# TensorE takes its rows of x straight from the store at a register's address, instead of from VectorE's copies

## The reference, cut to what matters

```python
def _propagate(all_emb, rows, cols, vals):
    acc = all_emb
    x = all_emb
    for _ in range(N_LAYERS):                      # 3
        x = jax.ops.segment_sum(vals[:, None] * x[cols], rows, num_segments=N_NODES)
        acc = acc + x
    return acc / (N_LAYERS + 1)
...
users_emb = all_users[users] + _upsample_nearest(mm_users[users])
items_emb = all_items + _upsample_nearest(mm_items)
rating = users_emb @ items_emb.T
rating = rating + bias_user[users] + bias_item.T
return jax.nn.sigmoid(rating)
```

## Time and profile before

| | |
|---|---|
| median of the runs | 7006.35 us (6999.16 to 7008.19) |
| the profiled execution: span | 7404.3 us |
| mean granted TensorE clock in it | 0.665 |
| VectorE (DVE) busy | 6190.8 us, 84% |
| TensorE (PE) busy | 4555.1 us, 62% |
| ScalarE (ACT) busy | 4518.3 us, 61% |
| GpSimd (POOL) busy | 2314.9 us, 31% |

### The profile page before, as it was taken

The page is one execution under the profiler, slowest core; times in us unless marked ns, Lnnn a source line. Parts: engine busy times, 40 slices in busy tenths (PEclk is TensorE's granted clock), DMA queues, the critical chain, the costliest instruction groups (busy, mean ns, idle before and its releaser), DMA issues.

```text
span 7404.3 us, 186636 instructions
## 1 busy us (share of the span) xinstructions
PE 4555.1 (62%) x58016; PEld 3947.8 (53%) x58020; DVE 6190.8 (84%) x15385; ACT 4518.3 (61%) x10708; POOL 2314.9 (31%) x2100
## 2 busy tenths in 40 slices
PE   5300111037777777886666666788666666678879
PEld 4200111036666666885555555688555555568854
DVE  9999999988888888998777777899877777789970
ACT  0155444345555557997555555799655555579976
POOL 0144344024544441001555555100155555510000
PEclk9755555566766666665777777655577777755569
DMA  9400000025555555554444444455344444445536
GB/s 345 159 0 0 0 0 0 0 73 148 152 149 149 149 149 136 143 145 106 136 138 136 142 138 139 133 145 146 108 138 137 136 140 138 137 131 145 147 107 241
DMA packets 750539, 918.14 MB, mean 124 GB/s; under 512 B 71784, under 2 KB 607881, under 8 KB 750363
## 3 DMA queue, kind: packets, MB, share of 16 engines
q1 hardware_dynamic: 658540, 665.77, 33.3%
q0 software_dynamic: 91520, 250.84, 9.1%
q10 hardware_dynamic: 434, 1.05, 0.1%
HBM read 529.36 MB, written 388.09 MB: 124 GB/s over the span
## 4 chain that ended last, share of the span: by engine, by line
DVE 41%; issue 18%; DMA 11%; ACT 11%; PE 8%; another core or an unknown queue 5%; DVEq 3%; POOL 2%; SPq 1%; ACTq 0%; POOLq 0%
DVE ring L1172 12%; DMA ring<-posts 10%; DVE ring L1205 9%; ACT ring L633 5%; DVE ring L1201 4%; ACT ring L631 3%; PE psum L1457 3%; DVE store L990 3%; DVE store L988 2%; DVE total L820 2%; DVE store L998 2%; PE psum L1459 2%; DVE store L999 2%; POOL ring L714 2%
## 5 line engine op out<-in xcount | busy, mean ns | idle before, releaser
L621 ACT ACTIVATE ring<-ring 128x64 f32<-128x64 f32 x7584 | 2032.7, 340 | 1672.2 <-DVE ring L1172 1370.1
L1457 PE MATMUL psum<-ring 128*128 128x128 bf16 x15168 | 2259.1, 265 | 876.7 <-issue 411.8
L1457 PEld LDWEIGHTS psum<-ring 128*128 128x128 bf16 x15168 | 1838.0, 126 | 1159.0 <-issue 685.9
L743 POOL DMA_INDIRECT posts<-ring x1896 | 1851.5, 977 | 1826.8 <-ACT ring L621 1201.0
L1459 PE MATMUL psum<-ring 128*128 128x64 bf16 x15168 | 2189.9, 232 | 319.3 <-issue 313.5
L1459 PEld LDWEIGHTS psum<-ring 128*128 128x128 bf16 x15168 | 1708.8, 117 | 381.5 <-issue 378.9
L1172 DVE TENSOR_REDUCE ring<-psum 128x128 f32<-128x256 f32 x3792 | 1418.7, 416 | 6.6 <-remote 5.7
L1205 DVE TENSOR_SCALAR ring<-ring,lane_f 128x512 bf16<-128x512 bf16 x3792 | 1167.2, 350 | 0.0
L1201 DVE COPY ring<-store 128x384 bf16 x1896 | 510.7, 269 | 669.4 <-remote 531.4
L1494 PE MATMUL psum<-ring 128*128 128x64 bf16 x15168 | 1002.8, 244 | 0.0
L1494 PEld LDWEIGHTS psum<-ring 128*128 128x128 bf16 x15168 | 965.3, 167 | 0.0
(11 more groups left out here) (241 smaller groups left out, 4701.1 us busy)
## 6 DMA issues: line engine op xcount, KB each, us to landing
ring<-posts SPq DMA_DIRECT2D x474, 516.0 KB, 3.9
ring<-lanes_d SPq DMA_DIRECT2D x474, 512.0 KB
out<-ring SPq DMA_DIRECT2D x200, 250.0 KB, 2.0
posts<-store SPq DMA_DIRECT2D x2, 20640.0 KB, 115.8
posts<-store SPq DMA_DIRECT2D x2, 20124.0 KB, 88.6
posts<-ring POOLq DMA_INDIRECT x1896
ring<-runs_d SPq DMA_DIRECT2D x158, 128.0 KB
user_rows<-total SPq DMA_DIRECT2D x1, 1568.0 KB, 5.9
```

The costliest lines, as they stand in the source:

```text
L621: last = nc.scalar.activation(of, of, ACT.Copy, scale=vring[:, h, c * BLOCK + b:c * BLOCK + b + 1])
L743: pool.indirect_dma_start(out=posts[:, :], out_offset=bass.IndirectOffsetOnAxis(ap=dring[:, h, c:c + 1], axis=0), in_=msg[:, n, :], in_off ...
L1457: pe.matmul(psum[:, c, b * 2 * F:(b + 1) * 2 * F], of, parts[:, 0:2 * F], start=(k == 0), stop=False, skip_group_check=True)
```

## The change

VectorE's copies into `xt` go, and its register loads with them. TensorE loads the four addresses itself, at the first chunk of each group of four, and its matmuls take their moving operand from `xflat` at those addresses. The tiles `xt` are gone; their place in `ring` is not used otherwise.

```diff
-        xt = [ring[:, 2048 + s * XT:2048 + (s + 1) * XT].bitcast(BF16) for s in range(4)]
...
                 def send(i, first, final=False):
                     for h in range(2):
-                        _, at_x = nc.values_load_multi_w_load_instructions(
-                            super_x[0:1, bass.ds(i * 8 + h * 4, 4)], engines=(mybir.EngineType.DVE,), min_val=0,
-                            max_val=(SUPERS - 1) * 2 * XT, skip_runtime_bounds_check_because="the chip clamps each above")
                         for c in range(4):
                             n = h * 4 + c
                             dve.wait_ge(s_sent, i * 8 + (done + n + 1))
-                            nc.vector.tensor_copy(xt[c], xflat[:, bass.ds(at_x[c], 2 * XT)])
...
                     for n in range(8):
                         c = n % 4
+                        if c == 0:
+                            _, at_x = nc.values_load_multi_w_load_instructions(
+                                super_x[0:1, bass.ds(i * 8 + n, 4)], engines=(mybir.EngineType.PE,), min_val=0,
+                                max_val=(SUPERS - 1) * 2 * XT, skip_runtime_bounds_check_because="the chip clamps each above")
                         pe.wait_ge(s_hots, i * 8 + (done + n + 9))
                         pe.wait_ge(s_added, i * 8 + (done + n + 1))
                         for b in range(BLOCK):
                             for k in range(2):
-                                of, parts = hot[c][:, k, b * P:(b + 1) * P], xt[c][:, k * PARTS * F:(k + 1) * PARTS * F]
-                                pe.matmul(psum[:, c, b * 2 * F:(b + 1) * 2 * F], of, parts[:, 0:2 * F],
+                                of = hot[c][:, k, b * P:(b + 1) * P]
+                                pe.matmul(psum[:, c, b * 2 * F:(b + 1) * 2 * F], of, xflat[:, bass.ds(at_x[c] + k * XT, 2 * F)],
                                           start=(k == 0), stop=False, skip_group_check=True)
-                                last = pe.matmul(psum[:, c, (2 * b + 1) * F:(2 * b + 2) * F], of, parts[:, 2 * F:3 * F],
+                                last = pe.matmul(psum[:, c, (2 * b + 1) * F:(2 * b + 2) * F], of, xflat[:, bass.ds(at_x[c] + (k * XT + 2 * F), F)],
                                                  start=False, stop=(k == 1), skip_group_check=True)
```

## The result

The changed kernel takes **6781.3 us** (6774.88 to 6790.09, four runs) beside 7006.76 of the kernel before (four runs): 0.9678 of it, 95% interval 0.9665 to 0.9692, or 225 us less. That is inside the range of the prediction; its value was 6724. A second measurement of the same pair gave 6777.8 and 7006.4, ratio 0.9664 (0.9651 to 0.9677).

A forecast was written before the change was run, and what follows sets the result against it. VectorE was taken as the bound, TensorE second. Gains of 161 us in layer 0 and 173 in layers 1 and 2, less 52 for bursts, made 282 us: 7006 to 6724, range 6600 to 6930.

The forecast's parts named there:

- the forecast's lower bound: Smallest gain the forecast allowed, written 104 + 99 - 104 = 99 us, giving 6907.
- VectorE's copies, 0.17 us a chunk: VectorE, every layer: removing the copies saves 632 x 0.17 = 107 us per layer, with nothing hiding them.
- VectorE's load in layer 0, 54 us: VectorE's sequencer, layer 0: removing the register load saves 158 x 0.34 = 54 us, bounds 0 and 73.
- TensorE's load and addresses, hidden: TensorE, groups of four: load about 0.39 us, addresses up to 0.32 a chunk; hidden at full clock, partly exposed at half.
- the rival of TensorE as the bound at half clock: TensorE at 1.2 GHz: load and addresses fully exposed, groups gain nothing there; 102 us gained, 6904; chance 0.20.
- The group of 5.07 to 5.27 in layers 1 and 2: Four chunks, layers 1 and 2: 5.72 us becomes 5.07 at full clock, 5.27 at half; 173 us over 316 groups.
- The bursts, 104 us halved to 52: TensorE stall bursts: faster VectorE has 0.5 us less work in hand, about 204 times; half of 104 us given back.
- the rival on the bursts: Layers 1 and 2: TensorE's address instructions and loads might remove the bursts; 6512 at best, 6592 with half; chance 0.10.
- The slower rival, 7127: TensorE's sequencer held at each chunk: half-clock group 6.76 us against 5.72, +171 us or +329; 7127; chance 0.08.

The follow-up runs named there:

- the later copies: Changed kernel with, in layers 1 and 2, each group's three small copies and VectorE's scatter wait moved after the next group's first-chunk comparisons: 6691.3 us, 0.9546 of before.

## Why the prediction was right, and where not

**Sign and size.** Forecast -282 us, measured -225 (and -229). The forecast of faster came true where it was measured; on chip 0 the same change is slower by 156. Nothing in my rivals said that one kernel could go both ways. So luck has a part in the sign, since three of the four chips of the experiments had the stalls, and in the size, since errors of both signs cancel in it, as shown below. (In the forecast's lower bound, 104 + 99 - 104, the first term should be the 107 of layer 0's copies: 102 us, 6904.)

**VectorE's copies, 0.17 us a chunk.** Right for VectorE by itself: 1.36 became 1.19, and the group without scatters is 4.96 against 5.04. How much of the 225 us is theirs no run shows, as the copies were never put back where before is at 7007.

**VectorE's load in layer 0, 54 us.** The gap went: 72.9 us of "issue", 41.7 in the trace on chip 0, are 5.0, or 0.03 us a group where I had expected 0.15. But layer 0 as a whole gained 124 us and not 161, if before took 1246 there at 7006 too, as it did in its traces with stalls. A DMA is late next: the wait for `runs_d` before L1180 is 36.7 us, where the profile of before has 9.0. I had written that SP's loads come a little earlier and left it at that. They are asked for at the same point of the loop. Without scatters this wait is gone and layer 0 takes 1048 us, so the scatters have a part in it. It was the wait to price.

**TensorE's load and addresses, hidden.** 0.34 us and 44 ns, near the 0.39 and 46 of the earlier trace rows, and hidden where there are no stalls: VectorE waits for TensorE 4.3 us in layer 1. The Trainium skill, "Runtime: NRT & Kernel Launch", "Instruction fetch mechanics", gives 200 ns per register, an estimated 0.8 us for four; that is not what this trace shows: 0.337 at the median. At the lower clock pairs of matmuls start 0.16 us apart, as before (2082.74 to 2082.90). So the rival of TensorE as the bound at half clock fell here. It was never pressed at the pace of the forecast, though: a group took 6.01 us with the scatters, and without them the granted clock was 1.00. The full-clock share of some 0.72, against 0.48 in the profile of before, is no effect of the change alone: over the whole program the runs of before at 7006 have a granted clock of 0.698 to 0.707, the changed kernel 0.702 to 0.708, and on chip 0 layer 1 has 0.76 before and 0.74 after.

**The group of 5.07 to 5.27 in layers 1 and 2.** This step failed: 950/158 = 6.01. I had bounded GpSimd by how fast it issues scatters (1.27 us) and not by when they land. VectorE overwrites `dring` and the lanes of `msg` only when the scatters of the same group one body before are done. In the profile of before, with stalls and 7.6 us a group on average, this cost 7.3 us in layer 1; in that of the changed kernel 76, with 20 more before the comparisons and longer instructions. The run without scatters shows that this side takes 167 us of layer 1, the later copies win back 86 us in all. What it cost the kernel before at 7006 no trace shows. First halves of 1150 us, which I had forecast for layers 1 and 2 of the profile, were meant for one with stalls; it had none, and they took 950 and 961.

**The bursts, 104 us halved to 52.** Wrong in its reason. They go with the place of the run: none in layers 1 and 2 of the changed kernel's first trace, some 100 a layer on chips 0 and 2. By the differences, layers 1 and 2 gained together about 225 - 124 = 101 us in the measurement, which puts before at about 1006 a layer there, 6.4 us a group and not the 5.72 that I started from; what fills the difference isn't known. If before had no bursts there and its layer 0 took 1246, the sum was 52 us too low at this term, 173 - 101 = 72 too high at the groups and 161 - 124 = 37 too high in layer 0: the 57 us between forecast and result. This split is an estimate, the total is measured. The Trainium skill's rule in "NOTIFIC — the notification-queue block", "Overflow: three behaviours, one of which stalls the engine", which I set beside the rival on the bursts, is neither shown nor excluded as the source of the stalls: every timed run here, with and without them, has a recorded span, so there was none without recording to compare.

**The slower rival, 7127.** A slower kernel came about, on chip 0, but not by this rival's mechanism. With stalls single matmuls and weight loads come late, in layers 1 and 2 as much without address instructions (405 us of "issue" in layer 1) as with them (388). Only in layer 0 do the addresses cost what the shorter VectorE gains.

## What to carry to other kernels

When the bound engine gets faster, price the buffers' round trips: not how often a DMA can be issued, but when it lands against when its buffer is wanted again, at the new pace. And put a wait that gates a few small instructions behind long ones, so that the engine still has work while its sequencer waits: moving the wait behind two comparisons was worth 86 us. When a profile shows "issue" gaps on TensorE without a wait, or a span well above the timed runs, measure on more than one chip before trusting the sign: this change won 225 us without these gaps and lost 156 with them.

## What was not expected of the hardware

One program has more than one time: the kernel before took 7006 us on chip 11 and in the first measurement, and 7303, 7309 and 7393 on chips 0, 3 and 2. Each chip was met once, so chip and moment can't be told apart. The traces differ in SP too. Its loop instructions (ns min/median/max), changed kernel, in the measurement (6781 us) and then on chip 0 (7459 us):

```profile
L488 SPq FUSED_REGOPS  x237: 50/50/64, 1575.5 to 5873.5; - x119
...
L488 SPq COMPARE_BRANCH  x237: 40/45/59, 1578.4 to 5885.7; - x119
```

```profile
L488 SPq FUSED_REGOPS  x237: 3/50/717, 1578.2 to 6523.4; - x119
...
L488 SPq COMPARE_BRANCH  x237: 3/45/717, 1581.2 to 6539.4; - x119
```

A register instruction of 50 ns takes up to 717 on the one, at most 64 on the other, and TensorE's stalls are of similar length (0.54 and 0.55 us of idleness, 0.75 between starts). They show in the first halves; the second halves, and everything before 1586 us, are equal to within some 6 us in the traces with and without stalls. They are not bound to a place in the loop: in the trace of before they move from body to body. TensorE's own register instructions take the same time with stalls as without: the address instructions of L1456 have 37/44/51 ns in both traces, the register load 330/335/822 against 330/337/856. So it isn't shown that TensorE's sequencer is what is late. What delays SP and the matmuls, and whether it goes with the chip, stays open.
